# Front stage of an adaptive-layer-norm block: row statistics by ScalarE's accumulator in place of VectorE's BN_STATS

## What is computed

```python
def _layernorm(x, axis=-1, eps=1e-05):
    m = jnp.mean(x, axis=axis, keepdims=True)
    v = jnp.var(x, axis=axis, keepdims=True)
    return (x - m) / jnp.sqrt(v + eps)
...
    h = _layernorm(x, axis=-1) * (1 + ca) + sa
    x = x + ga * attn(h)      # causal conv + silu for q, k, v; chunked delta rule; short and long FIR; gates; two RMS norms
    h = _layernorm(x, axis=-1) * (1 + cb) + sb
    x = x + gb * ffn(h)       # routed experts
```

## Time and profile before

| | |
|---|---|
| runs (3), us | 1031.11, 1034.27, 1034.35; median 1034.27 |
| profiled execution, us | 1034.05, of which the span (first to last instruction) 1032.3 |
| mean granted clock of PE over the span | 0.897 of 2.4 GHz |
| busy: PE, DVE, ACT, POOL | 816.8, 776.1, 457.4, 131.3 us |
| front stage | 26 to about 600 us of the span |
| iterations with statistics or modulation (i = -6 to 6) | 26 to about 373 us |

### The profile page before, as it was taken

One profiled execution on the slowest core, in us unless ns is written; L12 is line 12 of the kernel. 1 busy time (PEld: TensorE's weight loads), 2 busy tenths in 40 slices (PEclk: granted clock), 3 DMA queues, 4 the chain that ended last, 5 costly groups with the idle time before them and its releaser, 6 DMA issues. The chain is left out here.

```text
span 1032.3 us, 43867 instructions
## 1 busy us (share of the span) xinstructions
PE 816.8 (79%) x19697; PEld 514.0 (50%) x19697; DVE 776.1 (75%) x1683; ACT 457.4 (44%) x868; POOL 131.3 (13%) x179
## 2 busy tenths in 40 slices
PE   3889999989899889999655566979887309686886
PEld 2344565555555555555555454545443105454586
DVE  7265998988989889999978449998988365554462
ACT  4687656556656556555310203556566311111100
POOL 2000000000000000000000000101111037777100
PEclk9999999999999899999976666988887858988999
DMA  3400111110110101010000029444453223444444
GB/s 114 72 32 22 33 40 34 41 50 29 50 35 30 39 29 40 24 40 30 30 14 14 24 65 307 123 116 117 108 131 61 56 64 93 94 90 92 110 125 126
DMA packets 95907, 70.77 MB, mean 69 GB/s; under 512 B 18232, under 2 KB 82408, under 8 KB 95720
## 3 DMA queue, kind: packets, MB, share of 16 engines
q1 hardware_dynamic: 88680, 61.41, 21.4%
q0 software_dynamic: 4928, 5.51, 2.9%
q10 hardware_dynamic: 2112, 1.05, 0.3%
HBM read 40.00 MB, written 27.93 MB: 66 GB/s over the span
## 5 line engine op out<-in xcount | busy, mean ns | idle before, releaser
L715 PE MATMUL ps_p<-hT,Wconv 128*128 128x512 f32 x384 | 191.7, 628 | 7.9 <-PEq L114 7.1
L823 DVE TENSOR_TENSOR f_L<-f_L,f_prod 128x60 f32<-128x60 f32 (+14 forms) x240 | 121.3, 505 | 8.3
L820 DVE TENSOR_TENSOR f_prod<-f_L 128x60 f32<-128x60 f32 (+14 forms) x240 | 118.7, 495 | 6.0
L715 PEld LDWEIGHTS ps_p<-hT,Wconv 128*128 128x128 f32 x384 | 69.4, 194 | 79.5 <-issue 73.8
L1455 POOL DMA_INDIRECT got<-xh_dram,slot_row x64 | 61.8, 966 | 54.1 <-POOLq L1309 34.9
L1532 ACT ACTIVATE act_g<-pe_g 128x512 f32<-128x512 f32 x32 | 17.4, 595 | 113.6 <-PE pe_g L1502 113.6
L1480 PE MATMUL pe_x<-ident,got 128*128 128x128 f32 x64 | 12.3, 325 | 59.9 <-DMA got<-xh_dram,slot_row 59.9
L529 POOL COPY f_v_pad<-f_v_pad 128x32 f32<-128x32 f32 x15 | 4.5, 297 | 395.2 <-ACT f_v_pad L616 395.2
L681 PE MATMUL ps_a<-f_TT,f_r 32*32 32x64 f32 x2048 | 39.6, 242 | 18.6 <-DVE f_r L851 9.9
L681 PEld LDWEIGHTS ps_a<-f_TT,f_r 32*32 32x32 f32 x2048 | 36.7, 123 | 28.1 <-issue 17.8
L1159 PE MATMUL b_ps_y<-b_v_rest,fir 32*32 32x64 f32 x768 | 42.3, 286 | 3.6 <-DMA b_v_rest<-v_tok_dram 3.6
(11 more groups left out here) (323 smaller groups left out, 2062.1 us busy)
## 6 DMA issues: line engine op xcount, KB each, us to landing
w<-in_L_ffn_w_dram SPq DMA_DIRECT2D x48, 128.0 KB, 2.4
s_tok_dram<-f_s_tok SPq DMA_DIRECT2D x16, 256.0 KB, 2.0
o_tok_dram<-f_o_tok SPq DMA_DIRECT2D x16, 256.0 KB, 2.1
b_s_in<-s_tok_dram SPq DMA_DIRECT2D x16, 256.0 KB, 2.9
b_o_in<-o_tok_dram SPq DMA_DIRECT2D x16, 256.0 KB, 3.5
b_x_in<-_attn_hidden_states_dram SPq DMA_DIRECT2D x64, 64.0 KB, 2.1
out_dram<-b_x SPq DMA_DIRECT2D x64, 64.0 KB, 1.8
xh_dram<-b_xh SPq DMA_DIRECT2D x64, 64.0 KB, 1.8
```

Of the source, the lines that this page charges most:

```text
L715: last = pe.matmul(ps[:, :], g.Wconv[:, which, tap, :], tokens(t, tap), start=(tap == 0), stop=(tap == TAPS - 1))
L820: dve.tensor_tensor(tmp, M[:, :, m + 1:, m:m + 1].broadcast_to([P, 2, rows, cols]), M[:, :, m:m + 1, 0:cols].broadcast_to([P, 2, rows, col ...
L823: dve.tensor_tensor(M[:, :, m + 1:, 0:cols], M[:, :, m + 1:, 0:cols], tmp, ALU.add).then_inc(s["solved"], 1)
```

## The change

DVE no longer makes the statistics. ACT copies each 128x128 block of the tile onto itself with an accumulated output (row sums), DVE turns the four sums into minus the mean by one TENSOR_SCALAR, and ACT squares x about the mean with an accumulated output (sums of squares, written to `squares`; the squares themselves go to `xh` and are overwritten later). The root then takes `squares` with a scale of 1/128. The copies stand after the normalisation, ahead of the copies of q and k by heads; the squares stand after the modulation, ahead of the dense copy.

```diff
-        st, mv = k.sb("f_st", [P, 4, 6]), k.sb("f_mv", [P, 4, 2])
+        sums, minus, squares = k.sb("f_sums", [P, 4]), k.sb("f_minus_mean", [P, 4]), k.sb("f_squares", [P, 4])
...
-                    act.activation(dev[:, :], mv[:, :, 1], ACT.Sqrt, bias=g.eps_ln[:, :]).then_inc(s["ln_root"], 1)
+                    act.activation(dev[:, :], squares[:, :], ACT.Sqrt, bias=g.eps_ln[:, :], scale=1.0 / D).then_inc(s["ln_root"], 1)
...
+                n1 = tile(i + 6)
+                if n1 is not None:
+                    act.wait_ge(xs_in[n1 % 2], 16 * (n1 // 2 + 1))
+                    need(act, s["ln_mean"], n1 - 1)
+                    for m in range(4):
+                        last = act.activation(x_in[n1 % 2][:, m, :], x_in[n1 % 2][:, m, :], ACT.Copy, accum_out=sums[:, m:m + 1])
+                    last.then_inc(s["ln_sum"], 1)
                 if unit(i + 4) is not None:
                     t4 = i + 4
                     need(act, s["ga_ps"], t4 - 1)
...
                     last.then_inc(s["h_ready"], 1)
+                if n1 is not None:
+                    need(act, s["ln_mean"], n1)
+                    need(act, s["x_ps"], n1 - 1)
+                    for m in range(4):
+                        last = act.activation(xh[:, m, :], x_in[n1 % 2][:, m, :], ACT.Square, bias=minus[:, m:m + 1], accum_out=squares[:, m:m + 1])
+                    last.then_inc(s["ln_var"], 1)
                 if t is not None:
                     need(act, s["dense_ps"], t)
...
-                    dve.scalar_tensor_tensor(shift[:, :], mv[:, :, 0], -1.0, rstd[:, :], ALU.mult, ALU.mult).then_inc(s["ln_ready"], 1)
+                    dve.tensor_tensor(shift[:, :], minus[:, :], rstd[:, :], ALU.mult).then_inc(s["ln_ready"], 1)
...
-                    dve.wait_ge(xs_in[n1 % 2], 16 * (n1 // 2 + 1))
+                    need(dve, s["ln_sum"], n1)
                     need(dve, s["ln_ready"], n1 - 1)
-                    need(dve, s["ln_root"], n1 - 1)
-                    for m in range(4):
-                        dve.bn_stats(st[:, m, :], x_in[n1 % 2][:, m, :]).then_inc(s["ln_step"], 1)
-                    need(dve, s["ln_step"], 4 * n1 + 3)
-                    for m in range(4):
-                        last = dve.bn_aggr(mv[:, m, :], st[:, m, :])
-                    last.then_inc(s["ln_var"], 1)
+                    dve.tensor_scalar(minus[:, :], sums[:, :], -1.0 / D, None, ALU.mult).then_inc(s["ln_mean"], 1)
```

More of the change, by code:

```diff
@@ L427, in stage_front @@
         ps_a, ps_b = (stack.enter_context(nc.psum_tensor(n, [P, 2 * W], FP)) for n in ("ps_a", "ps_b"))
-        names = """ln_step ln_var ln_root ln_inv ln_ready xh_ready x_ps h_ready halo_ready
+        names = """ln_sum ln_mean ln_var ln_root ln_inv ln_ready xh_ready x_ps h_ready halo_ready
                    k_ps v_ps q_ps f0_ps f1_ps dense_ps dense_ready sm_ps silu_k silu_v silu_q square_k square_q gelu_0 gelu_1
```

## The result

| | before | after |
|---|---|---|
| runs, us | 4: 1030.73 to 1034.35, median 1032.69 | 4: 1046.05 to 1053.1, median 1050.01 |
| ratio of the two, 95% interval | | 1.0166 [1.0123, 1.0209] |
| profiled execution, us (span) | 1034.05 (1032.3) | 1053.1 (1051.4) |
| busy PE, DVE, ACT, us | 816.8, 776.1, 457.4 | 826.3, 764.7, 488.2 |

The change costs 17.3 us by the medians. 1048.7 was forecast, so the sign, the size and the range hold. DVE lost 11.4 us of busy time (12 forecast), ACT gained 30.8 (33 forecast), and the kernel became slower. Of the 19.1 us between the two spans 15.6 lie in the front stage. The back stage, whose code is the same, took 2.7 us longer, but its length went from 199.3 to 206.5 us over the twelve profiles of this document, so that part is not read as an effect of the change.

What follows compares the result with a forecast made beforehand. The front was taken as bound by a chain through ACT's dense copy, which PE and DVE await. Profiled 1034.05 us plus 12.6 (start-up 6.7, steady part 5.9) plus 2 for the clock gave 1048.7 us, range 1040 to 1059.

Steps and rivals of the forecast that it cites:

- Prices: Queue time per tile: on ACT four copies 1.2 us and four squares 1.55 us; on DVE a saving of 1.0 us.
- Rivals 2: On ACT, accumulator reads don't overlap: squares 2.3 us, copies 1.9 us a tile, total 1060 us; chance 0.13.
- 3 (hidden reads): On ACT, accumulator reads are cheap: squares 1.15 us, copies 0.8 us a tile, total 1041 us; chance 0.12.
- Start-up: Front iterations -6 to -1: copies and squares make PE 7.2 us late, of which 6.7 us is left.
- Steady part: Front iterations 0 to 5: +0.55 us in each odd one, +1.4 us in each even one, together 5.9 us.
- DVE wins 1.0 before L956: Iterations 0 to 5: DVE gains 1.0 us before its o transpose, then the squares take 1.55 us, leaving +0.55.
- The clock term: Longer PE idle stretches before the sm matmul bring two more clock falls than now: 2 us (bounds 0 and 8).
- price of a fall: One fall of PE's clock after idling before the sm matmul costs the chain 1 to 1.7 us.
- rival 1: Clock: most of the ten longer PE idle stretches end in a slow sm matmul, 12.6 + 8, 1055 us; chance 0.2.
- The chain: End of an iteration: PE's sm matmul and DVE's transpose wait for ACT's dense copy, so squares before it delay the stage.
- Rival 4, DVE decides: With the dense copy off the chain, DVE, relieved of 1.0 us in i = -2 to 5, ends 8 us sooner: 1026; chance 0.04.
- Regimes: Front stage: in iterations -6 to -2 DVE waits for the others, in 0 to 5 it is nearly full.

Runs made afterwards that it cites:

- tiles 0 to 5 only: The change for tiles 0 to 5 alone, tiles 6 to 11 with DVE's statistics as in before: ratio 1.0101 to before.
- Squares behind the dense copy: The changed kernel with the block of four squares moved past the dense copy: 1036.91 us against 1034.35 for before, ratio 1.0028.
- the relief alone: The kernel before with DVE's statistics replaced by one small instruction writing constants, nothing added on ACT: 1023.95 us, ratio 0.9874 to before.
- the filled kernel: The changed kernel with two constant matmuls in PE's idle time before the sm matmul, iterations 1 to 6: 1040.48 us against 1035.48 for before, 1.0074.
- second profile: The changed kernel run again unaltered, in a later group: 1049.58 us against 1032.33 for before, ratio 1.0125.
- ACT's gap: Before, with tiles 6 to 11 done by ACT, copies and squares moved into its wait ahead of silu q: 1026.51 us against 1034.35, 0.9929.
- tiles 6 to 11 only: The change for tiles 6 to 11 alone, tiles 0 to 5 with DVE's statistics as in before: ratio 1.0063 to before.
- squares only: The kernel before with four accumulating squares added on ACT ahead of the dense copy, result unused, DVE's statistics kept: 1057.22 us, ratio 1.0204.
- copies only: The kernel before with four accumulating copies added on ACT ahead of the q and k copies, result unused, DVE's statistics kept: 1039.52 us, ratio 1.0046.
- before filled: The kernel before with one constant matmul in PE's idle time before the sm matmul, iterations 1 to 6: 1035.58 us against 1035.48, ratio 0.9995.

## Why the prediction was right

- *Prices.* Read from one pair of Exps, a row of another stage and another width, and right: an accumulating ACTIVATE costs its successor 0.29 us (copy) or 0.38 (square with a bias pointer), since the read overlaps on both sides. Rivals 2 (no overlap) and 3 (hidden reads) fall by this.
- *Start-up.* The steps of the delay of after are 2.7, 1.5, 1.5 and 0.7 us (i = -4 to 0); 1.2 + 1.1, 1.55, 1.55 and 0.7 were forecast. In the first step the clock has a part (0.92): with tiles 0 to 5 only, where it was 1.00, the step is 2.2. The 1.1 us of the end of i = -5 show in the wait before the sm matmul of i = -4, 1.84 us in place of 0.78, and not in its start, which the luck of each run's first matmuls covers. Squares behind the dense copy shows that nothing else delays i = -3 to 0.
- *Steady part.* 5.9 us forecast, 6.7 and 8.1 found, but differently made. By the instructions alone it is 3.3 us, 0.7 in an even iteration (1.4 forecast) and 0.4 in an odd one (0.55). The step that was mis-sized is "DVE wins 1.0 before L956": the relief alone gives 1.5 us in the even iterations.
- *The clock term was too small.* "I take two more than now, which gives 2 us (bounds 0 and 8)": the filled kernel puts it at 5 to 9 us by the ratios. By the iteration lengths it is about 3 us (after) and 5 us (second profile) in the steady part, before's own falls taken off, and 0.4 and 3.5 us in the start-up: estimates, from two executions that were the slowest of their groups. The forecast's price of a fall, 1 to 1.7 us, fits (1.1 us in the steady part, 1.5 in i = -2); it is their number that was too low, and the sm pairs don't even show all of them. Slow sm pairs from i = -2 to 5 are one in before, two in after and five in its second profile. The mechanism of rival 1 thus was at work, for a part of its size.
- *Luck.* The chain is what was forecast, and squares behind the dense copy shows it. That the total came within 1.3 us of the median is luck: the instructions of the steady part cost 2.6 us less than worked out, and the clock cost more. How the 13 to 17 us split exactly stays open, as the falls differ from one execution to the next.
- *Rival 4, DVE decides*, fell for the change and is true a few lines off. Its condition was that the squares cost the chain less than 1.0 us a tile. Behind the dense copy they do in the steady part, where the delay shrinks (from 3.1 to 0.9 us), and in ACT's gap they cost nothing that can be seen: the delay falls by 8.0 us from i = 0 to 6, with the relief alone by 7.6. The Trainium skill's advice (Perfetto Trace Analysis, Identifying the Most-Contended Engine) to begin with the busiest engine is borne out here by relief only, at 0.9874; it says nothing of where the work taken off DVE may be put, and that decided the sign.
- *Regimes.* Both halves of the tiles lose. The late half costs 5 to 7 us (5.9 in the sum), the early one 10 (6.7 in the sum), and its profile puts the excess into iterations with a lower clock and one stall.

## What to carry to other kernels

Before moving work to an engine with spare time, look in its queue for the place: here with the squares ahead of an instruction that two engines wait for the kernel was 13 to 17 us slower, with them behind it 3 us, and with the work of the last six tiles in a wait of that engine 7 us faster. An engine's busy share says neither. The relief was worth something only in the iterations where the relieved engine is full: with the relief alone nothing before iteration 0 got shorter. And a longer wait ahead of TensorE was dearer here than its length, since the matmuls behind it often ran at half the clock, which cost the chain 1.1 to 1.6 us each time in most cases. When you price such a thing, compare the same iteration of two kernels, at the full clock and without a stall in both.

## What the runs showed of the hardware

- **The clock's falls are not a matter of one wait's length.** Sm pairs were slow after waits of 2.77, 3.19 and 3.31 us, but not after 2.85 in before (275.73) or 2.65 in after (219.37); in the second profile of after one was slow after 2.54 (92.73) where the same wait of 2.55 had left the first profile's fast. With tiles 6 to 11 only one was fast after 3.54 (347.73), and with the squares behind the dense copy one slow after 0.91 (212.16). Both levels can be seen in the pair: 1.10 us at the full clock, 2.05 at the half.
- **A slow pair is not the only sign of a fall.** In before the clock was 0.51 from 243.60 to 247.10, right behind the fast sm pair at 242.30, and the iteration took 33.42 us in place of 32.44. In after it was 0.50 from 183.20 to 184.30, while PE still waited for the dense copy. The granted clock of whole iterations shows all of it, and also that two profiles of one kernel differ: 0.97 in both from i = 0 to 6, but 1.00 and 0.94 in i = -2. A fall cost 1.5 us there (25.56 against 24.06), 1.1 in the steady iterations of the change, and 0.6 with the squares behind the dense copy (iteration 2: 32.23 at 0.95, iteration 0: 31.66 at 1.00).
- **Stalls of PE in the middle of the u matmuls** come in some executions and not in others. One in iteration 10, long after the last statistics:

```profile
486.15 0.49 PE L694 MATMUL ps_a<-f_TT,f_r 32*32 32x64 f32 x18 [1.83 <-issue]
486.57 3.40 PE L728 MATMUL ps_p<-hT,Wconv 128*128 128x512 f32 x4
```

PE waits 1.83 us for nothing that the profile shows, and the projection behind takes 3.40 us instead of 1.99 (granted clock 0.56). It moves the end of the front by some 4 us (delay of after from 12.3 to 16.1 in the next iteration). It is in the profiles of after, squares only (1.56 us, and the projection fast), copies only and before filled, and not in those of before, the second after, relief only or tiles 6 to 11 only, so it belongs to no kernel. The same matmuls stalled in iteration 2 of copies only and of tiles 0 to 5 only (1.61 us) in iteration 4 of after filled (1.87), and in iteration 7 of seven profiles, that of before among them (1.2 to 1.8). Its cause was not tried. One kernel's runs lie up to 14 us apart (before: 1028.35 to 1042.39 in 28 runs); the stalls and the falls are parts of that, how large is not shown. Effects under 5 us needed a dozen runs each.
